# A chunked recurrent attention kernel: output products of each level on one half of the array instead of the whole

## What is computed

```python
x = x + 0.5 * ffn(layernorm(x))        # ternary weights: clip(round(w / mean|w|)), sigmoid(x1) * x2
x = x + attention(layernorm(x))
x = x + 0.5 * ffn(layernorm(x))
```

```python
gt = exp(g_t); bw = b_t[:, :, None] * w_t
Sk = Sk * gt[:, :, None, :] + k_t[..., :, None] * bw[:, :, None, :]
Sv = Sv * gt[..., None] + bw[..., None] * v_t[:, :, None, :]
a  = softmax(einsum('bhd,bhdm->bhm', q_t, Sk) * SCALE)
o_t = einsum('bhm,bhmd->bhd', a, Sv)
```

## Time and profile before

| | |
|---|---|
| median of 3 runs | 2805.76 us (2805.7 to 2805.86) |
| span of the profiled execution, first to last instruction | 2799.8 us |
| TensorE products | 2752.0 us busy, 98% of the span, 13814 records |
| TensorE weight loads | 1934.3 us, 69% |
| VectorE | 2228.7 us, 80% |
| ScalarE | 1670.5 us, 60% |
| GpSimd | 1424.5 us, 51% |
| granted TensorE clock, mean | 0.999 |

### The profile page before, as it was taken

The page is one execution under the profiler, slowest core; times in us unless marked ns, Lnnn a source line. Parts: engine busy times, 40 slices in busy tenths (PEclk is TensorE's granted clock), DMA queues, the critical chain, the costliest instruction groups (busy, mean ns, idle before and its releaser), DMA issues. The chain is left out here.

```text
span 2799.8 us, 43437 instructions
## 1 busy us (share of the span) xinstructions
PE 2752.0 (98%) x13814; PEld 1934.3 (69%) x13814; DVE 2228.7 (80%) x5777; ACT 1670.5 (60%) x3777; POOL 1424.5 (51%) x2122
## 2 busy tenths in 40 slices
PE   6999899999999999999999999999999999999999
PEld 5888566666666666666666666666666666667887
DVE  7554688988888889888888888888888998884553
ACT  5111676777677677776767777766777776761110
POOL 0200466666566666665666666656666666661000
PEclk9999999999999999999999999999999999999999
DMA  4500211111112111111121111111211111115000
GB/s 169 195 16 16 79 35 35 35 50 35 50 35 72 50 57 35 49 35 50 35 72 50 57 35 50 35 50 35 80 50 57 36 53 35 50 29 192 15 16 31
DMA packets 90931, 151.06 MB, mean 54 GB/s; under 512 B 9296, under 2 KB 30928, under 8 KB 90192
## 3 DMA queue, kind: packets, MB, share of 16 engines
q1 hardware_dynamic: 90704, 148.29, 16.5%
HBM read 127.02 MB, written 21.23 MB: 53 GB/s over the span
## 5 line engine op out<-in xcount | busy, mean ns | idle before, releaser
L945 POOL TENSOR_TENSOR s<-s,tmp 128x256 f32<-128x256 f32 (+1 forms) x448 | 366.9, 819 | 303.2 <-DVE tmp L1262 284.4
L1608 PE MATMUL ps<-rows_even,standing 128*128 128x512 f32 x1024 | 496.5, 593 | 2.7 <-ACTq L1062 2.7
L1608 PE MATMUL ps<-hT,standing 128*128 128x512 f32 x1024 | 497.4, 593 | 0.0
L945 POOL TENSOR_TENSOR X<-S,D 128x256 f32<-128x256 f32 x384 | 275.7, 718 | 108.5 <-ACT S L1121 82.6
L1653 PEld LDWEIGHTS ps<-Y,S 128*128 128x128 f32 x1536 | 222.7, 193 | 150.2 <-issue 133.8
L341 ACT ACTIVATE sig<-up_ps 128x512 f32<-128x512 f32 x88 | 52.6, 598 | 390.3 <-PE up_ps L570 390.3
L1641 PEld LDWEIGHTS ps<-AM,XT 128*128 128x128 f32 x1536 | 216.5, 191 | 94.6 <-issue 90.1
L945 POOL TENSOR_TENSOR Y<-aT,D 128x256 f32<-128x256 f32 x384 | 280.4, 751 | 0.0
L945 POOL TENSOR_TENSOR A<-ident,dg 128x512 f32<-128x512 f32 x64 | 66.7, 1041 | 392.1 <-DVE standing L1348 367.1
L1262 DVE TENSOR_TENSOR tmp<-ps,D 128x256 f32<-128x256 f32 (+1 forms) x448 | 197.0, 440 | 84.7 <-PE ps L1641 69.0
L1354 DVE COPY_PREDICATED A<-standing,ps 128x256 f32<-128x256 int32 x448 | 236.3, 528 | 12.8 <-DVE A L1354 2.6
(11 more groups left out here) (215 smaller groups left out, 6824.2 us busy)
## 6 DMA issues: line engine op xcount, KB each, us to landing
standing<-in_wk_dram SPq DMA_DIRECT2D x64, 256.0 KB, 2.6
standing<-in_ww_dram SPq DMA_DIRECT2D x64, 256.0 KB, 2.6
standing<-in_wq_dram SPq DMA_DIRECT2D x64, 256.0 KB, 2.6
standing<-in_wv_dram SPq DMA_DIRECT2D x64, 256.0 KB, 2.7
standing<-in_wo_dram SPq DMA_DIRECT2D x64, 256.0 KB, 3.3
wq_dram<-wq SPq DMA_DIRECT2D x3, 2816.0 KB, 20.0
space<-in_w_dram SPq DMA_DIRECT2D x8, 704.0 KB, 11.0
x_sb<-in_x_dram SPq DMA_DIRECT2D x4, 1024.0 KB, 5.5
```

What stands on the lines that cost most here:

```text
L945: return nc.gpsimd.tensor_tensor(out, in0, in1, op)
L1608: mm = nc.tensor.matmul(bank[x][:, :], ck_(slot[x], kk), hT[n // NH % 2][:, kk, :], start=(kk == 0), stop=(kk == KT - 1))
```

## The change

Each product of 128 sources by 128 targets is made as two products of 64 sources (j = 0, 1) by 64 targets. The sources are columns 0 to 63 and 64 to 127 of the block, and the results go to PSUM partitions 0 to 63 and 64 to 127. For the built program this makes each of the new instructions one for an array of 128 rows by 64 columns, at column 0 or at column 64; every other product and transpose of the program is one for 128 by 128. The 64 targets are those of the blocks with which these 64 sources can pair: for l below 64, 32 columns from each of the two halves of the pair, for l = 64 all 64 from one. The parts of the bank that no product writes any more are masked out in the merge, as before. The calls, their order, their waits and the one semaphore count of each stay as they are.

```diff
--- before.py
+++ after.py
@@ -685,6 +685,24 @@
 def odd_targets(t, i):
 
     return pat(t, 1 + i * P, (HALF - 1, 2), (2, P // 2))
+
+
+def rows_pat(t, p0, p1, at, *dims):
+
+    part = t[p0:p1, :]
+    return bass.AP(part.tensor, part.offset + at, [list(part.ap[0])] + [list(d) for d in dims])
+
+
+def target_half(t, l, i, j, rows=(0, P)):
+
+    if l == 64:
+        return rows_pat(t, *rows, j * P + i * (P // 2), (1, P // 2))
+    return rows_pat(t, *rows, i * (P // 2) + j * (P // 4), (P, 2), (1, P // 4))
+
+
+def odd_target_half(t, i, j):
+
+    return pat(t, 1 + i * P + j * (P // 2), (HALF - 1, 2), (2, P // 4))
 
 
 def level_one(t):
@@ -1650,9 +1668,12 @@
 
                 def outputs(l, done):
                     for i in range(2):
-                        last = nc.tensor.matmul(pair_columns(bank[f"a2_{l}"], i), ck_(S[l], i),
-                                                odd_targets(aT, i) if l == 1 else pair_columns(Y[l], i),
-                                                start=True, stop=True)
+                        for j in range(2):
+                            half = (j * (P // 2), (j + 1) * (P // 2))
+                            last = nc.tensor.matmul(target_half(bank[f"a2_{l}"], l, i, j, half),
+                                                    ck_(S[l], i)[:, half[0]:half[1]],
+                                                    odd_target_half(aT, i, j) if l == 1 else target_half(Y[l], l, i, j),
+                                                    start=True, stop=True)
                     last.then_inc(done, 1)
 
                 def chunk_outputs(done):
```

## The result

The changed kernel takes 2834.06 us (median of four runs, 2831.69 to 2836.61) against 2805.81 of the kernel before in the same comparison: a ratio of 1.0105, with a 95% interval of 1.0092 to 1.0117. It is slower by 28 us, 1.0%, in the direction of the forecast and at about a quarter of its size (102 us).

What follows compares the result with a forecast made beforehand. TensorE's stream was taken to bound the kernel in the steady attention phase. Span 2799.8 + 176.5 (division changes) - 74.6 (overlap) = 2901.7, plus 6.0 from span to median, gave 2908 us; range 2735 to 2985.

Steps and rivals of the forecast that it cites:

- What bounds the kernel: In the steady attention phase TensorE's own stream sets the span; TensorE is busy 98% of the whole span.
- Term 2, the changes of division: Around output products, 760 switches between whole-array and half-array work cost 0 to 176.5 us; upper end taken.
- the run-out: At each division change TensorE lets the previous product finish completely, 0.164 us, a record's duration less its step.
- The bare loads: Unhidden weight loads at division changes: 0.05 us going in; going out 0.10 before projections, 0.06 before transposes.
- Term 1, the overlap: In the 448 output-product calls, left and right array halves work simultaneously: 74.6 us off, bounds 0 and 99.
- starts stay in order: Within a call, records start in program order L L R R, so eight take five steps, 0.278 us, not 0.444.
- changes cost, halves overlap: The forecast's own case for the output products: 2850 to 2960 us by itself, chance 0.36.
- Rival (a): Output products: division changes free, halves overlap, some gain lost to merge waits; 2737 to 2757, say 2747; chance 0.34.
- Rival (b): Output products: division changes cost 176.5 us and nothing overlaps; 2982 us; chance 0.16.
- Rival (c): Output products: free changes, no overlap, small products follow at half a step; 2806, up to 2812; chance 0.10.
- (d): Output products: each of 3584 records waits 0.05 us for its unhidden load; 179 us, so 2985; chance 0.04.
- What would show it: Profile signs: calls of 0.28 us, following projection 0.26 us later, TensorE idle tens of us, busy share below 1.00.

Runs made afterwards that it cites:

- the faster order with three groups: Half-array calls of levels 1, 2, 4 together, 8 alone, 16, 32, 64 together, against the kernel before: 2780.12 us, ratio 0.9908.

## Why the prediction was right or wrong

**What bounds the kernel** was right. TensorE's stream is the span: what the runs added to or took from it came out in the total, within 8 us, until three groups were left. The 6.0 us that the sum carries from span to median are partly one fast execution, as said above; since the same 6.0 is added back to the same span, the forecast of 2908 doesn't depend on it.

**Term 2, the changes of division**, was right as a mechanism and too large. The step that failed is the run-out: "a record's duration less its step", 0.164 us, taken as what the engine waits for. (Of its two readings, "275" for 128 columns isn't in the earlier trace rows, where these products have 277; 2 ns change nothing.) The end of a record is modelled in the profile, and it is not the moment from which the next division may start. Going in cost 0.09. The fixed part of a group is 0.15, of which 0.05 is its bare first load, so the run-out on the way out cost 0.10. The bare loads, read from the engine at rest, were right: 0.11 and 0.05 measured against 0.10 and 0.06. With 0.095 for 0.164 the term is 760 x 0.069 = 52 us smaller: 124 instead of 176.5. The load queue shows the same: it rests 0.76 us ahead of each group, since no load of the new division starts under a product of the old one. So the Trainium skill's rule (TensorEngine Tiling (Array Packing), "Key Properties") that a change of tiling mode drains TensorE agrees with this trace in that nothing of the new mode starts, not even a load; the price here was 0.09 to 0.10 us each way besides the bare load.

**Term 1, the overlap**, was too small. "Two records of one half can't overlap, a record of the other half can" holds, but "starts stay in order" doesn't: four steps remain of eight, 0.23 us and not 0.278, so 95.9 us and not 74.6. The run with the loops exchanged shows it, up to the 0.04 us that one half fell behind in groups of two calls. The upper bound of the term, 99 us, was nearly reached. That a second call in a group costs four steps and not five would have come out with starts in order too, since its first record could run beside the last one of the call ahead of it; the term counted five for all 448.

Together: 176.5 - 52 and 74.6 + 21 turn + 101.9 into + 29. Both errors made the forecast too slow. The case was named rightly (changes cost, halves overlap), its size was not: 2834 lies below the 2850 to 2960 that the forecast gave this case by itself, and only the wide range of all cases holds it. I had taken the upper end of one bound and the in-order value of the other; the middle of the first, 88 us, would have given + 14.

**Rival (a)**, faster, was given 0.34. Its point of decision was right in kind: at 95.9 us of overlap a change must cost less than 95.9 / 760 = 0.126 us, and it costs 0.165 with its load. The wait that it priced, for the merge of level 4 ahead of level 16, did not come even in the faster order with three groups: the four projection records ahead of that group take 1.81, no more than their streams and the change. **Rival (b)** had no overlap in it and falls with the run on one half. **Rival (c)** and **(d)** fall: the halves overlap, and loads inside a group are hidden (0.23 for eight records, with the moving columns alone as the pace).

**What would show it** named TensorE's busy share falling below 1.00 and its idle going "to tens of us". Neither came: 600.00 of 600, and 1.6 us idle. A wait for the run-out lies under the tails of records, and is to be read from starts.

## What to carry to other kernels

In this kernel half-array products in pairs took half the time where stationary and moving columns were both halved, but each group of them cost a fixed price at its two ends, here 0.35 us, as much as 1.6 calls gain. So before tiling the array, count the groups and not the products, put what is to be tiled side by side, and then look for the engine that is now reached too early. Price a change of mode by the step from start to start; the duration of a record overstates it, and the busy share hides it.

## What the runs showed of the hardware that I had not expected

- The two column halves don't wait for each other's turn within a call: with four records of the left half issued ahead of four of the right, eight records still took 0.39 us, against 0.61 with all eight on one half. With two such calls in a row one half fell 0.04 us behind.
- A change from 128 to 64 columns or back costs 0.09 to 0.10 us of standstill after the stream of the last product, less than the 0.164 us by which a record outlasts its step, and it is about the same behind a 512-column product (0.092 us) and behind a 64-column one (0.098).
- At the two sizes run, the moving columns set the pace of half-array fp32 products with 64 stationary columns: 0.23 us for eight records of 64 columns and 0.43 for eight of 128.
